# The tail of an embedding, state-space and expert kernel with tokens on partitions: normalisation by statistics per token, residual added where the shared expert's result leaves PSUM

## The reference, cut to what matters

```python
h = tok(x)                                  # shifted patches @ W + b
h = concatenate([h, txt], axis=1)           # 16 x 324 x 192
h = h + mamba(layernorm(h))                 # 16 layers, then rmsnorm(out) * final_norm_w
n = layernorm(h)
scores = sigmoid(n @ gate_weight.T)         # 16 experts, each takes its 648 best tokens
shared = silu(n @ Ws_g.T) * (n @ Ws_u.T) @ Ws_d.T
h = h + scatter_of_experts(n, scores) + shared
```

## Time and profile before

| what | value |
|---|---|
| median of 3 runs | 13483.69 us (13472.51 to 13488.46) |
| the profiled execution: its own time | 13473.85 us |
| the profiled execution: span of the core | 13472.1 us, mean granted TensorE clock 0.979 of full speed |
| busy share of the span | PE 89%, DVE 93%, ACT 83%, POOL 91% |
| embedding | 0 to 144.7 us |
| 16 layers | to 12442.6 us |
| stage A | to 12582.8 us |
| stage B | to 12777.5 us |
| placing, then experts | to 12859.7 us, then to 13472.1 us |

### The profile page before, as it was taken

The page is one execution under the profiler, slowest core; times in us unless marked ns, Lnnn a source line. Parts: engine busy times, 40 slices in busy tenths (PEclk is TensorE's granted clock), DMA queues, the critical chain, the costliest instruction groups (busy, mean ns, idle before and its releaser), DMA issues. The chain is left out here.

```text
span 13472.1 us, 200925 instructions
## 1 busy us (share of the span) xinstructions
PE 12055.9 (89%) x53560; PEld 6552.2 (49%) x53560; DVE 12559.0 (93%) x7301; ACT 11225.6 (83%) x23472; POOL 12295.6 (91%) x3794
## 2 busy tenths in 40 slices
PE   7888899898989888988988888888898998898899
PEld 5444444444444444444444444444444444444776
DVE  4999999999999999999999999999999999999543
ACT  4988888898888989898998989898988989898311
POOL 3999999999999999999999999999999999999033
PEclk8999999999999999999999999999999999999889
DMA  4555555555555555555555555555555555555122
GB/s 131 161 168 160 167 162 162 167 166 168 163 167 160 165 161 162 166 162 167 163 173 161 169 162 159 166 162 166 161 166 162 165 164 168 165 166 164 43 61 69
DMA packets 794048, 2095.45 MB, mean 156 GB/s; under 512 B 97637, under 2 KB 382501, under 8 KB 791841
## 3 DMA queue, kind: packets, MB, share of 16 engines
q1 hardware_dynamic: 697360, 1689.33, 36.1%
q0 software_dynamic: 95808, 403.86, 15.3%
q10 hardware_dynamic: 720, 0.55, 0.0%
HBM read 1419.42 MB, written 288.73 MB: 127 GB/s over the span
## 5 line engine op out<-in xcount | busy, mean ns | idle before, releaser
L986 POOL TENSOR_TENSOR dbu<-dtu_rep,b_rep 128x1944 f32<-128x1944 f32 x2055 | 9328.6, 4778 | 72.3 <-DMA dtu_rep<-dtu_rows 72.3
L924 DVE TENSOR_TENSOR_SCAN h<-ps,dbu 128x972 f32<-128x972 f32 x4105 | 8668.5, 2160 | 174.9 <-POOL dbu L986 125.1
L702 ACT ACTIVATE ps<-dt_rep,A_cur 128x323 f32<-128x323 f32 x12315 | 5874.4, 520 | 825.9 <-DVE h L924 775.3
L519 PE MATMUL ps<-h,fold 128*32 128x486 f32 x16408 | 3785.8, 582 | 357.9 <-DVE h L932 246.3
L932 DVE TENSOR_TENSOR h<-h,ps 128x1944 f32<-128x1944 f32 (+1 forms) x1795 | 3336.3, 1870 | 52.3 <-PE ps L506 25.6
L995 POOL TENSOR_TENSOR h<-h,c_rep 128x972 f32<-128x972 f32 (+1 forms) x769 | 2712.4, 3527 | 1.7 <-DVE h L924 1.2
L519 PEld LDWEIGHTS ps<-h,fold 128*32 128x32 f32 x16408 | 783.7, 110 | 2331.6 <-issue 1628.9
L603 PE MATMUL ps<-u_raw,w_cv 128*128 128x162 f32 (+7 forms) x8256 | 1800.8, 371 | 2.6 <-ACT terms L746 1.3
L603 PEld LDWEIGHTS ps<-u_raw,w_cv 128*128 128x128 f32 x8256 | 1358.5, 190 | 547.5 <-issue 206.2
L552 PE MATMUL ps<-x_norm,w_z 96*128 96x324 f32 (+1 forms) x4128 | 1053.8, 401 | 279.9 <-ACT x_norm L792 238.0
L590 PE MATMUL ps<-x_norm,w_u 96*128 96x324 f32 (+1 forms) x4144 | 994.7, 383 | 232.0 <-ACT x_R L733 228.3
(11 more groups left out here) (189 smaller groups left out, 11801.6 us busy)
## 6 DMA issues: line engine op xcount, KB each, us to landing
dt_rep<-dt_rows SPq DMA_DIRECT2D x1028, 486.0 KB, 5.2
dtu_rep<-dtu_rows SPq DMA_DIRECT2D x1028, 486.0 KB, 5.2
sums<-terms POOLq DMA_DIRECT2D x258, 972.0 KB, 6.7
b_rep<-b_rows SPq DMA_DIRECT2D x1030, 162.0 KB, 3.5
sums<-sums POOLq DMA_DIRECT2D x258, 486.0 KB, 4.7
dt_rows<-sums SPq DMA_DIRECT2D x258, 486.0 KB, 2.9
dtu_rows<-terms SPq DMA_DIRECT2D x258, 486.0 KB, 3.2
c_rep<-b_rows SPq DMA_DIRECT2D x771, 162.0 KB, 5.5
```

The source lines that it names most:

```text
L519: mm = pe.matmul(y_ps[32 * r:32 * r + 32, half, :], fold[:, :], flat(h, step)[:, half * YW:(half + 1) * YW], start=(s < NR), stop=(s == la ...
L702: ins = act.activation(decay[s % 2][:, it * L + 1:(it + 1) * L], dt_rep[:, s % NR, it, 1:L], ACT.Exp, scale=A_cur[:, it * N + s:it * N + s ...
L924: dve.tensor_tensor_scan(flat(h, s), decay[s % 2], flat(dbu, s), 0.0, ALU.mult, ALU.add).then_inc(s_scan, 1)
L986: pool.tensor_tensor(steps(dbu, s, 2), steps(dtu_rep, r, 2), each(b_rep[:, q, :], 2), ALU.mult).then_inc(s_dbu, 1)
```

## The change

`h_rows` becomes 108 x 9216, tokens on partitions. In the embedding ACT copies each turned sequence from PSUM to one of two new tiles `tok_h` before its Ln, and SP stores that, one sequence at a time, waiting for the copy.

Stage A keeps tokens on partitions throughout. ACT squares one group ahead; Ln and Exp work on 108 x 12 tiles, one for a group. DVE multiplies by the root and by the weight (`fw`, now a row repeated on 108 partitions) in place in `x_R`; POOL, idle here before, adds the residual; DVE takes bn_stats and bn_aggr and writes normalised tokens to `f_ntok` (four buffers). SP stores these to `n_rows` from here, in pieces of 192 and 64 columns. PE turns `f_ntok` to features on partitions, ACT evicts it to `nrm`, PE multiplies by the gate. The sums with ones, the squares, `x_T` and `two` are gone. ACT goes through seven rounds of two table loads instead of five.

In stage B `down` is the expert's product alone, the turning back and ACT's three evictions are gone, and DVE evicts: half of PSUM plus the residual in `x_R`, 108 x 192, as the last thing of a step.

```diff
@@ embed_and_norm
+                def store(b):
+                    sp.wait_ge(s_kept, b + 1)
+                    sp.dma_start(h_rows[:, b * ROW:(b + 1) * ROW], h_tok[b % 2][:, :, :].rearrange("p c d -> p (c d)")
+                                 ).then_inc(s_st[b % 2], 16)
...
                     if i >= N_EDGE + 2:
-                        store(i - 2)
...
+                        store(2 * (i - N_EDGE - 2))
+                        store(2 * (i - N_EDGE - 2) + 1)
+                for b in range(B - 4, B):
+                    store(b)
...
                 def root(b):
                     act.wait_ge(s_mom, b + 1)
                     wait(act, s_nrm, b - 1)
+                    wait(act, s_st[b % 2], 16 * (b // 2))
+                    act.copy(h_tok[b % 2][:, 0:2, :].rearrange("p c d -> p (c d)"), turned[:, 2 * (b % 2), 0:2 * H])
+                    act.copy(h_tok[b % 2][:, 2, :], turned[:, 2 * (b % 2) + 1, 0:H]).then_inc(s_kept, 1)
@@ scores_and_norm
+                def store(b):
+                    sp.wait_ge(s_nrm, b + 1)
+                    rows = n_rows[b * L:(b + 1) * L, :].rearrange("(s p) d -> p s d", p=TS)
+                    sp.dma_start(rows[:, :, 0:H], n_tok[b % GS][:, :, :]).then_inc(s_st[b % GS], 16)
+                    sp.dma_start(rows[:, :, H:256], n_tok[b % GS][:, :, 128:H]).then_inc(s_st[b % GS], 16)
...
+                for b in range(B):
+                    turn(b)
+                    if b % GS > 0:
+                        gate(b - 1)
+                    if b % GS == GS - 1:
+                        gate(b)
...
+            @block.gpsimd
+            def _(pool):
+                for b in range(B):
+                    pool.wait_ge(s_scaled, b + 1)
+                    pool.wait_ge(s_h[b % RES], 16 * (b // RES + 1))
+                    pool.tensor_tensor(row(b), row(b), res[b % RES][:, :], ALU.add).then_inc(s_stream, 1)
...
+                squares(0)
+                for k in range(N_G + 3):
                     act.preload_act_table_set(LOG_SET)
...
+                    if k < N_G:
+                        log_x(k)
+                    if 2 <= k < N_G + 2:
+                        log_n(k - 2)
                     act.preload_act_table_set(MAIN_SET)
...
+                    if k < N_G:
+                        root_x(k)
+                    if 2 <= k < N_G + 2:
+                        root_n(k - 2)
+                    if k + 1 < N_G:
+                        squares(k + 1)
+                    if 2 <= k < N_G + 2:
+                        for b in range(GS * (k - 2), GS * (k - 1)):
+                            evict(b)
+                            if b > GS * (k - 2):
+                                exp_gate(b - 1)
+                        exp_gate(GS * (k - 1) - 1)
...
+                def scale(b):
+                    dve.wait_ge(s_rsx, b // GS + 1)
+                    for c in range(TPL):
+                        at = b * TPL + c
+                        ins = dve.scalar_tensor_tensor(out=piece(b, c), in0=piece(b, c), scalar=rs_x[:, at:at + 1],
+                                                       in1=fw[:, :], op0=ALU.mult, op1=ALU.mult)
+                    ins.then_inc(s_scaled, 1)
...
+                for k in range(N_G + 2):
+                    if k < N_G:
+                        for b in range(GS * k, GS * (k + 1)):
+                            scale(b)
+                            if b > GS * k:
+                                measure(b - 1)
+                        measure(GS * (k + 1) - 1)
+                    if 1 <= k <= N_G:
+                        for b in range(GS * (k - 1), GS * k):
+                            normalise(b)
+                    if k > 1:
+                        sigmoid(k - 2)
@@ shared_and_choice
-                    for c in range(2):
-                        pe.matmul(p_down[k % 2][:, c * HC:(c + 1) * HC], x_T[:, c, at:at + TS], two[:, :],
-                                  start=(c == 0), stop=False)
                     for it in range(SF):
-                        pe.matmul(p_down[k % 2], av[b % 2][:, it, s * TS:(s + 1) * TS], w_d[:, it, :],
-                                  start=False, stop=(it == SF - 1))
-                    for c in range(2):
-                        mm = pe.transpose(p_n[k % 2][:, c * HC:(c + 1) * HC], nrm[:, c, at:at + TS], ident[0:HC, 0:HC])
+                        mm = pe.matmul(p_down[k % 2], av[b % 2][:, it, s * TS:(s + 1) * TS], w_d[:, it, :],
+                                       start=(it == 0), stop=(it == SF - 1))
...
+                def evict(k):
+                    b, s = k // 3, k % 3
+                    dve.wait_ge(s_dn, k + 1)
...
+                    dve.scalar_tensor_tensor(out=o_tok[b % 2][:, s, :], in0=p_down[k % 2], scalar=0.5, in1=x_R[:, at:at + H],
+                                             op0=ALU.mult, op1=ALU.add).then_inc(s_cp, 1)
...
                     chore(k)
+                    if k >= 4:
+                        evict(k - 4)
@@ lay_out
-        "fw": a["L0_attn_final_norm_w"].reshape(2, HC).T,
+        "fw": np.broadcast_to(a["L0_attn_final_norm_w"][None, :], (TS, H)),
```

More of the change, by code:

```diff
@@ L143, in embed_and_norm @@
         rs = [sb(f"tok_rs{i}", [TS, TPL]) for i in range(2)]
+        h_tok = [sb(f"tok_h{i}", [TS, TPL, H]) for i in range(2)]
         s_w = [sem(f"s_tokw{q}") for q in range(4)]
@@ L1362, in _, with turn, gate @@
             def _(pe):
[L1363 to L1387 removed]
+                def turn(b):
+                    pe.wait_ge(s_nrm, b + 1)
+                    wait(pe, s_ev, 2 * (b - 1))
+                    for half in range(2):
+                        for c in range(TPL):
+                            mm = pe.transpose(turned(b, half)[:, c * TS:(c + 1) * TS],
+                                              n_tok[b % GS][:, c, half * HC:(half + 1) * HC], ident[0:TS, 0:TS])
+                        mm.then_inc(s_turn, 1)
+                def gate(b):
+                    pe.wait_ge(s_ev, 2 * b + 2)
+                    wait(pe, s_ge, b - 3)
                     for s in range(TPL):
@@ L1447, in root_n, with squares @@
-                def root_n(b):
-                    act.wait_ge(s_lnn, b + 1)
-                    act.activation(rs_n[b % GS][:, :], rs_n[b % GS][:, :], ACT.Exp, scale=-0.5).then_inc(s_rsn, 1)
+                def squares(g):
+                    wait(act, s_sq, g)
+                    for b in range(GS * g, GS * (g + 1)):
+                        for c in range(TPL):
+                            at = b * TPL + c
+                            ins = act.activation(square[:, at % (GS * TPL), :], piece(b, c), ACT.Square, accum_out=ss_x[:, at:at + 1])
+                    ins.then_inc(s_sq, 1)
@@ L1451, in exp_gate, with root_n, evict @@
+                def root_n(g):
+                    act.wait_ge(s_lnn, g + 1)
+                    act.activation(group(rs_n, g), group(rs_n, g), ACT.Exp, scale=-0.5).then_inc(s_rsn, 1)
+                def evict(b):
+                    for half in range(2):
+                        act.wait_ge(s_turn, 2 * b + half + 1)
+                        act.copy(nrm[:, half, b * L:(b + 1) * L], turned(b, half)).then_inc(s_ev, 1)
                 def exp_gate(b):
@@ new lines, in measure @@
+                def measure(b):
+                    dve.wait_ge(s_stream, b + 1)
+                    wait(dve, s_mom, b - 1)
+                    for c in range(TPL):
+                        ins = dve.bn_stats(stats[b % 2][:, c, :], piece(b, c))
+                    ins.then_inc(s_stat, 1)
+                    dve.wait_ge(s_stat, b + 1)
+                    for c in range(TPL):
+                        ins = dve.bn_aggr(moments[:, b * TPL + c, :], stats[b % 2][:, c, :])
+                    ins.then_inc(s_mom, 1)
@@ L1568, in shared_and_choice @@
         p_down = [ps[0:TS, 4 + i, 0:H] for i in range(2)]
-        p_n = [ps[0:TS, 4 + i, H:2 * H] for i in range(2)]
         p_pos = [ps[0:TS, 7 - i, 0:3 * 128] for i in range(2)]
```

231 lines of the change are left out of this document (75 added, 156 removed).

## The result

| what | before | after |
|---|---|---|
| median | 13478.1 us (4 runs) | 13662.1 us (4 runs, 13639.0 to 13681.7) |
| ratio | | 1.0137, 95% interval 1.0118 to 1.0155 |
| the profiled execution: own time, span | 13473.85, 13472.1 us | 13681.74, 13679.9 us |
| embedding, to DVE's first operation of the layers | 144.7 us | 149.6 us |
| 16 layers, from there to ACT's first square of stage A | 12297.9 us | 12568.5 us |

What follows compares the result with a forecast made beforehand. Layers: DVE and POOL busy 98%, unchanged; stage A a chain between engines; stage B bound by PE. Terms 6 - 38 - 27 = -59 give 13415, some 5 higher for the median: 13420 us, range 13395 to 13448.

Steps and rivals of the forecast that it cites:

- the one for the embedding's copies: Embedding: two ACT copies per sequence, 0.8 us together, with room on ACT, DVE and PE; SP's next load 3.2 us late.
- the prediction's own sign of being wrong: Layers expected within 15 us of 12297.9; the prediction called itself wrong if they move.
- slower after all: Layers: larger fw shifts HBM data, landings get later; slower by over 0.2% from 0.34 us per unit, 13535 at 0.45; chance 0.05.
- Embedding, +6 forecast: Embedding: later loads cost 5 us over five loads, the last store 1; together +6 us, range 2 to 13.
- the last store: Embedding's end: last store goes out after the copies, lands 0.4 to 2.3 us after DVE's old end; 1 us taken.
- Stage A, 102 forecast: Stage A: the rebuilt chain takes 102 us in place of 140.2, 38 us less.
- PE's clock: Stage A: PE's clock stays near 0.50; the full-clock rival had stage A at 90, the kernel at 13408, chance 0.09.
- the add: Stage A: POOL's residual add, 1.7 us taken between 1.33 and 2.85; first and last of a group show, 1.9 us.
- the row: Stage A: profile row where the next operation starts 0.02 us behind a 1.28 us table load; gain 38, not 27.
- Stage B, -27 forecast: Stage B: 48 steps lose the residual's matmuls and the turning back on PE; 27 us less, range 14 to 28.
- The new eviction: Stage B: DVE's 108x192 eviction, under 0.49 us, fits 0.87 us of waiting; rival where it hits the count's chain: 13434, chance 0.08.
- The rival lost: Stage A: DVE and POOL never overlap, a group takes 17 us for 12, stage A 121, time 13439; chance 0.12.

Runs made afterwards that it cites:

- the wide input alone: Kernel before with input fw enlarged from 96x2 to 108x192, of which it loads the same 96x2 values: 13485.2 us, ratio 1.0002.
- DVE's copies: Changed kernel with the embedding's two copies per sequence made by DVE behind its statistics in place of ACT: 13417.4 us, ratio 0.9947.
- 13427.6 (ACT's copies): Changed kernel with 8 idle semaphore increments on ACT ahead of its loop: 13427.6 us, ratio to the kernel before 0.9958.

## Why the prediction was wrong, step by step

**The step that failed** is the one for the embedding's copies, with the sentence ahead of the parts: "the change leaves every instruction of theirs as it is, so I look at the rest". The copies were costed at the time they take in the embedding (0.8 us a sequence, and "ACT, DVE and PE have room for this"). Right as far as it went: 0.48 and 0.32 us. The layers were put at no change, and the rival that doubted it was held down with "nothing in the layers' code moves". It did move: 32 instructions on ACT move what stands behind them, and ACT's loop had 4 places to spare. The cost fell in 127 turns, in a stage whose instructions the change does not touch. ACT waited 1.48 + 1.65 = 3.13 us in a turn, and the layers grew by 270.6 / 127 = 2.13 us in one. The rest is most likely hidden by decay steps that ACT makes ahead of DVE's scans; no run separates that. Layers that move were the prediction's own sign of being wrong, but nothing in the trace of before showed this wait. What could have been counted is the ACT code ahead of its loop and in it.

**The rival "slower after all"** (0.05) had the sign and the stage, but neither the size (0.45 us in a unit was its dearest price, 1.06 came) nor the cause. Its place, POOL's wait for HBM, did not move, and the wide input alone does nothing.

**Embedding, +6 forecast, +4.9 measured.** The load shown in the earlier trace rows went at 92.20 for 92.3 forecast, and PE waited for `patch_in` six times in place of two (waits of PE: us in total, times, the longest):

```profile
PE tok_acc L267 <- DMA patch_in<-in_patches: 24.0, 6, 20.7
```

The longest of these is the wait for the first load, as before. What the new order of loads and stores costs shows at DVE: its statistics waited 2.00 us for PE in the earlier trace rows and in each step beside it, and five times longer now, first here:

```profile
95.12 0.89 DVE L222 BATCH_NORM_STATS2 tok_stats<-tok_turned 108x6 f32<-108x192 f32 x3 [2.89 <-PE tok_turned L253]
...
149.61 0.87 DVE L1278 MEMSET ps<- 128x972 f32 x1 [1.82 <-PEq L166]
```

The five (2.89, 2.28, 2.78, 2.71, 2.28) are 2.9 us over 2.00 together, where 5 were taken. The wait for the block's end, in the second line, was 0.84 before: 1.0 more, as taken for the last store. The end of the embedding lies at 149.6 and 154.2 us in the two executions with ACT's copies, and at 144.7 to 150.6 (mean 147.1) in seven with the old embedding: about 5 more, inside the range of 2 to 13, with a scatter as large as itself.

**Stage A, 102 forecast, 98.9 measured** in both executions, 99.0 with DVE's copies. From the timeline, one group and the round behind it:

```profile
12725.61 3.20 DVE L1489 SCALAR_TENSOR_TENSOR x_R<-x_R,f_rsx,fw 108x192 f32<-108x192 f32 x6 [18.77 <-ACT f_rsx L1438]
...
12726.76 1.51 POOL L1419 TENSOR_TENSOR x_R<-x_R,f_res 108x576 f32<-108x576 f32 x1 [13.59 <-DVE x_R L1489]
12728.89 1.40 POOL L1419 TENSOR_TENSOR x_R<-x_R,f_res 108x576 f32<-108x576 f32 x1 [0.62 <-DVE x_R L1489]
...
12735.03 0.88 DVE L1497 BATCH_NORM_STATS2 f_stats<-x_R 108x6 f32<-108x192 f32 x3 [0.38 <-POOL x_R L1419]
...
12736.17 3.17 DVE L1489 SCALAR_TENSOR_TENSOR x_R<-x_R,f_rsx,fw 108x192 f32<-108x192 f32 x6
...
12746.70 3.54 DVE L1510 TENSOR_SCALAR f_ntok<-x_R,f_moments,f_rsn 108x192 f32<-108x192 f32 x12
...
12762.41 0.29 ACT L1442 ACTIVATE f_rsn<-f_moments,eps 108x12 f32<-108x12 f32 x1
...
12779.81 0.30 ACT L1442 ACTIVATE f_rsn<-f_moments,eps 108x12 f32<-108x12 f32 x1
```

The first scaling comes 7.5 us after the first square (7 forecast), the first normalisation 28.6 us after it (31), rounds are 17.4 us apart by Ln of the second root (17.5), and PE's clock is 0.50 as forecast. The over-estimate is the add: a group took DVE 10.56 us (12725.61 to 12736.17) for 12. DVE waited 0.38 us for an add in it, where the first and the last were to show 1.9, and an add took 1.466 us in the mean where 1.7 was taken. Behind a table load the next operation starts 0.01 to 0.02 us later here too, so the row was the better guide against the drain of the Trainium skill (ScalarE: Activation LUTs, "What ACT_TABLE_LOAD costs"), by which stage A would have taken 113.

**Stage B, -27 forecast, -26.4 measured.** The new eviction takes 0.35 us where 0.49 was taken, and DVE still waits for the count, 0.76 us in a step where 0.4 was expected and 1.47 stood before (groups by line, then one step):

```profile
L1694 DVE SCALAR_TENSOR_TENSOR f_otok<-g_ps,x_R 108x192 f32<-108x192 f32 x48 | 16.8, 350 | 2.7 <-PE g_ps L1617 2.3
```

```profile
12881.75 0.16 DVE L1707 SCALAR_TENSOR_TENSOR c_step<-g_ps,c_bit 128x1 int32<-128x1 f32 x1 [0.76 <-PE g_ps L1623]
```

PE stayed the bound, 164.0 of 168.3 us. In the other execution the stage took 172.8 at a mean clock of 0.94 for 0.97, so its length is known to some 4 us.

**The sum.** With the loop kept inside its blocks the change gives 13427.6 (ACT's copies) and 13417.4 us (DVE's) for 13420 forecast. The terms of the sum came out as +4.9, -41.3 and -26.4 for +6, -38 and -27 in the changed kernel's own profile; the term that was missing, taken as nothing, was four times the sum (13662 less 13420 is 242).

## What to carry to other kernels

Where an engine runs a loop of several hundred instructions, every instruction added ahead of it on that engine moves the loop in its code, and here three cost nothing and seven cost 1.3% of the kernel. So count the engine's instructions in the loop and ahead of it before costing an edit at its own time, and after an unexplained slowdown look for "issue" waits at the loop's head and for instruction packets in part 3 of the page. The cure is as cheap as the illness, for a loop that has a place where it fits: a few idle instructions, or the same work on an engine with a shorter loop.

## What the runs showed of the hardware

- A branch back into code that had to be fetched again left ACT idle at the loop's head for 1.28 to 4.42 us (means 1.47 in the changed kernel, 1.53, 2.27 and 2.22 with 31, 7 and 263 instructions of padding). From the branch to the loop's first instruction the trace has 2.4 to 5.2 us in these four runs and 0.24 to 0.28 in the six others. A second wait, five or six instructions on, cost 1.64 us in the mean in the changed kernel. The whole fetch is 5 packets of 8.2 KB a turn, 0.1% of the DMA engines' time: it is a delay, not a load.
- How much the kernel loses depends on where the seam lies: 270.6 and 242 us in the layers with a second wait (the changed kernel, and 31 instructions of padding), 181 and 189 without one, with 7 and 263. With 7, the one wait at the loop's head:

```profile
6140.27 1.44 ACT L702 ACTIVATE ps<-dt_rep,A_cur 128x323 f32<-128x323 f32 x3 [2.09 <-issue]
```

- DVE and POOL do get in each other's way in stage A, by turns. The three scalings of the second sequence lie under the add at 12726.76 and take about 2.1 of the 3.20 us shown above, where the three ahead of them take 1.07: one alone takes 1.55 us, nearly as long as the add, where the others take 0.41. In the third group the scalings kept their pace and the add took 2.17 for 1.40. The three statistics of a sequence, with one input, take 0.86 us with an add beside them (at 12733.44) and 0.88 without (at 12735.03). This agrees with the rule of the Trainium skill (GPSIMD Engine Reference, "Specifications") that DVE's instructions with two SBUF inputs contend with POOL. The rival lost because the order of DVE's work puts only the second sequence's scalings wholly under an add, a microsecond a group; the later ones meet its end and take 1.29.
